# A graph attention network on one core: transposes of the normalised rows moved from TensorE to the DMA crossbar, with a new order of the softmax and GpSimd steps

## What is computed

```python
h = relu(layernorm0(x))                       # no scale, no shift
for l in range(3):
    si = h @ attn_w[l, :256];  sj = h @ attn_w[l, 256:]
    scores = leaky(si[:, :, None] + sj[:, None, :] + attn_b[l])     # slope 0.2
    attn = softmax(where(mask, scores, -inf))                       # mask = adj + identity > 0
    h1 = layernorm(h + attn @ h, g1[l], beta1[l])
    ff = gelu(h1 @ W1[l] + b1[l]) @ W2[l] + b2[l]                   # 256 -> 1024 -> 256
    h = layernorm(h1 + ff, g2[l], beta2[l])
out = x + h
```

## Time and profile before

| what | value |
|---|---|
| median of three runs | 2402.7 us |
| profiled execution, its own time | 2401.22 us |
| span of its trace | 2399.4 us |
| TensorE busy | 97% of the span |
| ScalarE / VectorE / GpSimd busy | 79% / 78% / 71% |
| mean granted TensorE clock | 0.995 of full speed |
| slots | 96, of about 24 us each |

### The profile page before, as it was taken

One profiled execution on the slowest core, in us unless ns is written; L12 is line 12 of the kernel. 1 busy time (PEld: TensorE's weight loads), 2 busy tenths in 40 slices (PEclk: granted clock), 3 DMA queues, 4 the chain that ended last, 5 costly groups with the idle time before them and its releaser, 6 DMA issues.

```text
span 2399.4 us, 47629 instructions
## 1 busy us (share of the span) xinstructions
PE 2333.0 (97%) x16608; PEld 1649.3 (69%) x16608; DVE 1869.7 (78%) x5974; ACT 1892.0 (79%) x3498; POOL 1698.2 (71%) x1543
## 2 busy tenths in 40 slices
PE   3999999999999999999999999999999999999997
PEld 2667777776666777777666777777766677777775
DVE  6887777777888777777888787878788877787874
ACT  4878787878888878787888877778788887878783
POOL 3567676768887666667887767676878776767686
PEclk9999999999999999999999999999999999999998
DMA  5200000001211000001121000000121100000012
GB/s 162 87 28 27 1 1 2 1 19 41 93 62 36 1 1 1 1 1 36 54 78 60 23 2 1 1 1 2 53 67 63 41 2 1 1 1 1 19 42 65
DMA packets 77421, 70.83 MB, mean 30 GB/s; under 512 B 7040, under 2 KB 75648, under 8 KB 77184
## 3 DMA queue, kind: packets, MB, share of 16 engines
q1 hardware_dynamic: 77184, 67.79, 9.1%
HBM read 51.01 MB, written 16.78 MB: 28 GB/s over the span
## 4 chain that ended last, share of the span: by engine, by line
PE 66%; POOL 16%; DVE 11%; ACT 3%; issue 2%; POOLq 0%; DVEq 0%
PE p_pair L380 29%; PE p_hid L366 28%; PE p_pair L422 4%; PE p_pair L432 2%; POOL rstd L786 2%; DVE dots L613 2%; DVE g_lo L572 2%; POOL w_f L835 2%; POOL h_res L798 2%; POOL h_res L800 2%; POOL norm L812 2%; DVE res L675 2%; POOL w_f L828 2%; POOL X_lo L804 2%; POOL w_f L826 2%
## 5 line engine op out<-in xcount | busy, mean ns | idle before, releaser
L380 PE MATMUL p_pair<-w_hi,g_hi 128*128 128x256 f16 x3072 | 837.6, 273 | 0.0
L380 PE MATMUL p_pair<-w_lo,g_hi 128*128 128x256 f16 x3072 | 837.6, 273 | 0.0
L380 PE MATMUL p_pair<-w_hi,g_lo 128*128 128x256 f16 x3072 | 837.5, 273 | 0.0
L572 DVE TENSOR_TENSOR g_lo<-p_hid,g_hi 128x512 f16<-128x512 f32 x768 | 528.6, 688 | 396.2 <-ACT g_hi L483 389.7
L478 ACT ACTIVATE p_hid<-p_hid,b_eff 128x512 f32<-128x512 f32 x768 | 504.5, 657 | 316.9 <-PE p_hid L366 315.7
L798 POOL TENSOR_TENSOR h_res<-norm,g_rows 128x1024 f32<-128x1024 f32 x96 | 227.7, 2372 | 384.0 <-DVE res L675 377.3
L483 ACT ACTIVATE g_hi<-p_hid 128x512 f16<-128x512 f32 x768 | 458.6, 597 | 24.4
L366 PE MATMUL p_hid<-hT_hi,w_hi 128*128 128x512 f16 x1536 | 458.2, 380 | 1.5 <-DVE g_lo L572 1.4
L366 PE MATMUL p_hid<-hT_hi,w_lo 128*128 128x512 f16 x1536 | 458.3, 380 | 0.0
L366 PE MATMUL p_hid<-hT_lo,w_hi 128*128 128x512 f16 x1536 | 457.9, 380 | 0.0
L786 POOL TENSOR_TENSOR rstd<-var_eps,minus_half 128x4 f32<-128x4 f32 x224 | 242.2, 1081 | 259.0 <-DVE minus_mean L587 253.7
(11 more groups left out here) (68 smaller groups left out, 3658.5 us busy)
## 6 DMA issues: line engine op xcount, KB each, us to landing
x_in<-in_x SPq DMA_DIRECT2D x32, 512.0 KB, 4.1
w_f<-in_x SPq DMA_DIRECT2D x32, 512.0 KB, 5.8
out<-w_f SPq DMA_DIRECT2D x32, 512.0 KB, 4.2
adj_in<-in_adj SPq DMA_DIRECT2D x32, 256.0 KB, 4.5
w_f<-in_L_gnn_W SPq DMA_DIRECT2D x6, 1024.0 KB, 6.1
attn_rows<-in_L_gnn_attn_w SPq DMA_DIRECT2D x1, 768.0 KB, 5.9
g_rows<-in_L_gnn_g SPq DMA_DIRECT2D x2, 384.0 KB, 7.5
b_rows<-in_L_gnn_b SPq DMA_DIRECT2D x1, 384.0 KB, 6.7
```

Of the source, the lines that this page charges most:

```text
L380: mm = pe.matmul(ff_banks(s)[:, t, :], g[i][:, nodes], w[l][:, c, :], start=(c == 0 and t % 2 == 0 and n == 0), stop=(c == C - 1 and n == ...
L572: dve.tensor_tensor(g_lo[i][:], p_hid[k][:], g_hi[i][:], ALU.subtract).then_inc(g_lo_ready, 1)
```

## The change

The rows `norm1` are no longer transposed by TensorE. ScalarE copies them to fp16 `h_hi` (`high_h`, after step 3), GpSimd subtracts to get `h_lo` (`low_h`), and SyncE issues one transposing DMA of 256 KB for each (`turn_h`), from SBUF to SBUF, into `hT_hi` and `hT_lo`. `transpose_norm1`, `high_hT` and `split_hT` are gone. The score rows and the transposed probabilities lie in the two banks of the pair that the aggregate of the same item will use; `p_att` is gone, and its bank holds `p_rows`, a PSUM copy of the two attention vectors of the layer, which `dot_products` reads; it is refilled once in eight items. In the order of the work: `spread_sj`, `add_scores` and `row_maxima` go from step 4 to step 3, `exponentials` from step 5 to step 4, `high_X` from step 3 to step 1, `norm_input` is for item s+4; on VectorE `feed_statistics` goes from step 3 to 4 and the `aggregates` behind it from step 4 to 5, `dot_products` to step 4 and item s+3, `input_statistics` to step 1 and item s+5 with its `aggregates` at step 2; GpSimd's slot has a new order. The first slot is -5 instead of -4.

```diff
-FIRST_SLOT = -4
+FIRST_SLOT = -5
...
+            def turn_h(r, s):
+                i = s % 2
+                if later(r, s, 2):
+                    sp.wait_ge(hid_psum, total(r, s - 2, C, C))
+                for h, hT, made, turned in ((h_hi, hT_hi, h_hi_ready, hT_hi_ready), (h_lo, hT_lo, h_lo_ready, hT_lo_ready)):
+                    sp.wait_ge(made, total(r, s, 1, 1))
+                    sp.dma_start_transpose(hT[i][:].rearrange("p t k n -> p (t k) n"),
+                                           h[:].rearrange("p t d -> p (t d)")).then_inc(turned, 16)
...
-                if is_item(r, s + 2) and layer_of(s + 2) == 0 and group_of(r, s + 2) + 2 < G:
-                    sp.wait_ge(x0_ready, group_total(r, s + 2, 4, 4))
-                    load_x(group_of(r, s + 2) + 2)
+                if is_item(r, s + 3) and layer_of(s + 3) == 0 and group_of(r, s + 3) + 2 < G:
+                    sp.wait_ge(x0_ready, group_total(r, s + 3, 4, 4))
+                    load_x(group_of(r, s + 3) + 2)
...
+                if is_item(r, s + 1):
+                    turn_h(r, s + 1)
...
-                    if c == 4 and is_item(r, s + 1):
-                        transpose_norm1(r, s + 1)
-                    if c == 4 and is_item(r, s + 2) and not first:
+                    if c == 3 and is_item(r, s + 2):
                         spread_sj(r, s + 2)
...
+            def high_h(r, s):
+                act.wait_ge(norm1_ready, total(r, s, 4, 4))
+                if later(r, s):
+                    act.wait_ge(hT_hi_ready, total(r, s - 1, 16, 16))
+                act.activation(h_hi[:], norm1[:], ACT.Copy).then_inc(h_hi_ready, 1)
...
-                    if c == 3 and is_item(r, s + 2):
+                    if c == 3 and is_item(r, s + 1):
+                        high_h(r, s + 1)
+                    if c == 1 and is_item(r, s + 2):
                         high_X(r, s + 2)
-                    if c == 4 and is_item(r, s + 1):
-                        high_hT(r, s + 1)
-                    if c == 5 and is_item(r, s + 2):
+                    if c == 4 and is_item(r, s + 2):
                         exponentials(r, s + 2)
...
+                if q == 0 and pair == 0:
+                    dve.tensor_copy(p_rows[:], attn_rows[:, l]).then_inc(rows_ready, 1)
...
+                    if c == 1 and starts and not late:
+                        input_statistics(r, s + 5)
+                    if c == 2 and starts and not late:
+                        aggregates(0, group_total(r, s + 5, 10, 8))
...
                     if c == 4 and is_item(r, s - 1):
+                        feed_statistics(r, s - 1)
+                    if c == 5 and is_item(r, s - 1):
                         aggregates(2, total(r, s - 1, 10, 8))
-                    if c == 5 and is_item(r, s + 1):
-                        split_hT(r, s + 1)
...
+                    if c == 4 and is_item(r, s + 3):
+                        dot_products(r, s + 3, 0)
+                        dot_products(r, s + 3, 1)
```

More of the change, by code:

```diff
@@ L192, in gnn_kernel @@
         h_res = [sb(f"h_res{i}", [P, T, D]) for i in range(2)]
-        hT_hi = [sb(f"hT_hi{i}", [P, KD, TN], F16) for i in range(2)]
-        hT_lo = [sb(f"hT_lo{i}", [P, KD, TN], F16) for i in range(2)]
+        h_hi, h_lo = sb("h_hi", [P, T, D], F16), sb("h_lo", [P, T, D], F16)
+        hT_hi = [sb(f"hT_hi{i}", [P, T, KD, N], F16) for i in range(2)]
+        hT_lo = [sb(f"hT_lo{i}", [P, T, KD, N], F16) for i in range(2)]
         g_hi = [sb(f"g_hi{i}", [P, TN], F16) for i in range(GS_RING)]
@@ L238, in gnn_kernel @@
         x0_ready = sem("x0_ready")
+        rows_ready = sem("rows_ready")
         dots_ready = sem("dots_ready")
@@ L409, in transpose_probs @@
                 for t in range(T):
-                    mm = pe.transpose(p_att[:, t, :], probs[:, t, :], ident[:])
+                    mm = pe.transpose(pT_bank(s)[:, t, :], probs[:, t, :], ident[:])
                 mm.then_inc(pT_psum, 1)
@@ L424, in aggregate @@
                 mm.then_inc(agg_ready, 1)
[L426 to L434, removed]
             def slot(r, s):
@@ L553, in slot @@
                         copy_probs(r, s + 2)
-                    if c == 7 and is_item(r, s + 3) and layer_of(s + 3) == 0:
-                        norm_input(r, s + 3)
+                    if c == 7 and is_item(r, s + 4) and layer_of(s + 4) == 0:
+                        norm_input(r, s + 4)
             slots(act, slot)
@@ L630, in add_scores @@
                 for t in range(T):
-                    dve.scalar_tensor_tensor(out=scores[:, t, :], in0=p_att[:, t, :], scalar=s_i[q][:, t:t + 1],
+                    dve.scalar_tensor_tensor(out=scores[:, t, :], in0=sj_bank(s)[:, t, :], scalar=s_i[q][:, t:t + 1],
                                              in1=mask[q][:, t, :], op0=ALU.add, op1=ALU.add).then_inc(score_steps, 1)
@@ L700, in slot @@
             def slot(r, s):
-                starts = is_item(r, s + 4) and layer_of(s + 4) == 0
-                late = isinstance(r, int) and (r, s) == (0, -3)
-                if isinstance(r, int) and (r, s) == (0, -2):
+                starts = is_item(r, s + 5) and layer_of(s + 5) == 0
+                late = isinstance(r, int) and (r, s) == (0, -4)
+                if isinstance(r, int) and (r, s) == (0, -3):
                     dve.wait_ge(attn_dma, 2 * 16)
@@ L711, in slot @@
                         dve.wait_ge(stat_steps[1], total(r, s + 1, 10, 4))
-                    if c == 4 and is_item(r, s - 1):
+                    if c == 5 and is_item(r, s - 1):
                         dve.wait_ge(stat_steps[2], total(r, s - 1, 10, 4))
-                    if c == 6 and starts and not late:
-                        dve.wait_ge(stat_steps[0], group_total(r, s + 4, 10, 4))
-                    if isinstance(r, int) and (r, s, c) == (0, -2, 3):
+                    if c == 2 and starts and not late:
+                        dve.wait_ge(stat_steps[0], group_total(r, s + 5, 10, 4))
+                    if isinstance(r, int) and (r, s, c) == (0, -3, 1):
                         dve.wait_ge(stat_steps[0], group_total(0, 1, 10, 4))
@@ L800, in h_residual, with low_h @@
                 pool.tensor_tensor(h_res[i][:], h_res[i][:], rows(res_rows, l, T), ALU.add).then_inc(h_res_steps, 1)
+            def low_h(r, s):
+                pool.wait_ge(h_hi_ready, total(r, s, 1, 1))
+                if later(r, s):
+                    pool.wait_ge(hT_lo_ready, total(r, s - 1, 16, 16))
+                pool.tensor_tensor(h_lo[:], norm1[:], h_hi[:], ALU.subtract).then_inc(h_lo_ready, 1)
             def low_X(r, s):
@@ L848, in slot @@
                     norm_feed(r, s - 1)
-                if is_item(r, s - 2) and layer_of(s - 2) == L - 1:
-                    skip_connection(r, s - 2)
-                if is_item(r, s + 4) and layer_of(s + 4) == 0:
-                    inverse_deviation(s + 4, 0, group_total(r, s + 4, 10, 10), group_total(r, s + 4, 2, 1))
-                if is_item(r, s - 1) and not (isinstance(r, int) and PER * r + s == ITEMS):
-                    layer_output(r, s - 1)
             slots(pool, slot)
```

99 lines of the change are left out of this document (44 added, 55 removed).

## The result

The changed kernel takes **2632.5 us** (median of 4 runs, 2632.05 to 2633.59) against 2402.7 us before (4 runs, 2402.35 to 2403.58): ratio 1.0958, 95% interval 1.0944 to 1.0972. The profiled execution took 2632.3 us, its span is 2630.5 us. The forecast was 2612 us, and slower.

What follows compares the result with a forecast made beforehand. TensorE (97% busy) was taken to bound short slots, GpSimd and VectorE long ones. New rings: 66 x 25.47 + 24 x 28.65 = 2368.6 against 2166.3, +202; start and end +8; 2401.2 + 210 = 2611, said 2612, range 2555 to 2740.

Steps and rivals of the forecast that it cites:

- TensorE's work: TensorE per slot: without the eight transposes (0.87 us per item), 23.9 us falls to 23.0 us.
- The ring of the quiet slots: ScalarE, VectorE, GpSimd: exponentials delay g_lo and second aggregates at step 5; no slot shorter than 25.5 us where it closes.
- N: Start of norm_attention in slot s, taken as time zero for the walk through the new order.
- The ring of the long slots: Eight slots of 24, item s+5 of layer 0: GpSimd's input deviation waits for VectorE's step 2 aggregates; 28.65 us.
- The sum: 90 h_res intervals, items 5 to 95: 66 x 25.47 + 24 x 28.65 = 2368.6 us, +202.
- 15 us of possible gain: Long slots before the change: seven in each of three periods, 0.7 us each, if nothing but TensorE bound.
- Start and end: Five slots before item 5, where weights are prepared, and the end: +8 us, between 0 and 25.
- The edits costed at nothing: spread_sj and probabilities in pair banks, PSUM dot products, high_X at step 1, SyncE loads: zero cost, waits cover them.
- low bound: Transposing DMAs land like a plain 256 KB load, 4.5 us; even one after the other, no cost.
- their rival: Transposing DMAs land late, TensorE waits at the first hidden matmul: 2690 if two us late, high bound 3000; chance 0.20.
- The one in which only TensorE's ring holds: GpSimd's tail is shorter; ring P, X_hi, low_X, deviation, N: 23.8 us in 66 intervals, about 2500 us; chance 0.06.
- The faster one: Exponentials at step 4 hide, TensorE sets 23.0 us everywhere: 2304 us; chance 0.09.

Runs made afterwards that it cites:

- D: Changed kernel with VectorE's second-normalisation aggregates ahead of g_lo of step 5, and GpSimd's low_X behind the first deviation, input deviation behind h_residual: 2327.5 us.
- A: Changed kernel with VectorE's aggregates of the second normalisation moved ahead of its g_lo of step 5: 2527.6 us.
- B: Changed kernel with GpSimd's deviation of the first normalisation (item s+1) moved ahead of the input's: 2565.3 us.
- J: D with the five broadcast row loads one slot earlier on SyncE and item 0's dot products moved forward: 2326.4 us.
- I: D with both dot products reading the attention rows from SBUF and the copy into PSUM removed: 2491.7 us.
- H: Changed kernel with the transpose of h_lo issued twice in a row, first into a spare tile, TensorE waiting for both: 2632.3 us.
- F: D with ScalarE's exponentials put back from step 4 to step 5: 2365.2 us.

## Why the prediction was right, and where it was off

**TensorE's work.** 23.9 - 0.87 = 23.0 us per slot: D shows 23.02 once nothing else binds.

**The ring of the quiet slots.** From N = 410.00 the links came at: gelu of step 3 +1.99 (forecast 1.98), h_hi done +4.19 (4.2), scores' maxima done +5.73 (5.76), gelu of step 5 +10.75 (10.74), its g_lo +12.15 (12.07), GpSimd's power +13.46 (13.39) after a wait of 2.32 (2.3). Slot 25.56 (25.47). Nothing in it is an average: each term was a row of the same operations in the old order, and so they added up. A removed the link, and this ring no longer set the slot.

**The ring of the long slots.** 28.49 (28.65); B opened it and the quiet slots did not move. The wait for the input's statistics, on which the walk rests, is there: 0.94 us ahead of the input's power.

**The sum.** 90 intervals: 2374.4 (2368.6). The 60 quiet slots are 0.1 us longer than I had them, the 24 long ones 0.15 shorter, and six slots that I counted as quiet take 26.27 us, two in each period (1462.99 to 1489.26). In reading the trace of before I said that seven slots of 24 are longer; they are eight, six of 24.67 us and two of 24.54, and only in the six has GpSimd both the skip connection and the input's deviation. The sum did not use this count, but the 15 us of possible gain there are 18. In the six slots of 26.27 us VectorE makes a mask and nothing is done for an input. GpSimd, then VectorE, of the changed kernel in such a slot:

```profile
1471.20 0.74 POOL L789 TENSOR_TENSOR shift<-minus_mean,rstd 128x4 f32<-128x4 f32 x1
1472.04 2.33 POOL L817 TENSOR_SCALAR norm<-res,rstd,shift 128x256 f32<-128x256 f32 x4
```

```profile
1471.21 0.66 DVE L605 CUSTOM_DVE_ANT_0 adj_in<-eye_i,adj_in 128x1024 uint16<-128x1024 uint16 x1
```

The shift takes 0.74 us instead of 0.20 and ends just behind the mask's operation, the norm 2.33 instead of 2.16: 0.71 us, which is the excess of these slots over 25.57. Six times that are 4 us on the ring.

**Start and end**, the term that was mis-sized: +8 (0 to 25), measured 31.4 - 8.4 = +23.0. I had counted only the five slots with weights. Those gave 14.5 (from item 0's h_res to item 5's: 149.5 against 135.0), but item 0's own h_res came 16.9 later, 62.33 against 45.43: TensorE's first work is at 28.5 instead of 19.0, and the first slot is one earlier (-5). That the added lead-in slot is the cause is argued, not shown: J brought TensorE's first work back to 18.4 and item 0's h_res by only 2.1 us. The 15 us by which this term was too small are the greater part of 2632 - 2612.

**The edits costed at nothing.** The dot products from PSUM took 474 and 417 ns on average (482 and 423 from SBUF before, where they stood elsewhere), X_hi was ready 1.5 us ahead of low_X (1.7 said), and TensorE was idle ahead of spread_sj for 19.8 us in all. What I did not see is what they were for: read from SBUF at their new place, the dot products cost 164 us in D's order (I).

**The transposes.** They landed after 3.1 us, below my low bound of 4.5, and their rival falls (H). 256 KB in 3.1 us are 85 GB/s, from issue to landing. The Trainium skill, Advanced Engine Details and Errata, section X-Bar Transpose (TRN2), has transposing DMAs as fast as copies; the trace does not speak against that, since the plain 256 KB loads from HBM landed after 4.4 us. Its 350 to 400 GB/s, by which the prediction made it under 1 us, are not reached at this size. The Trainium skill, VectorE: DVE Perf Modes, section The three transpose paths, gives 1309 ns for a 128x128 block; the eight of one DMA took 3.1 us together, so they do not follow each other at that price, and the 10.5 us that the prediction weighed do not arise.

**The rivals.** The one in which only TensorE's ring holds was put at 2500 and given 0.06; A has such slots (24.05 against 23.8, long ones 28.5). The faster one, at 2304 with the aggregates named as the link most likely to be loose, is what D comes to at 2327. Of the 23 us between the two, 18 are the 24 long slots, which take 23.78 us and not 23.0, and 3 are the start and end. Loosening that one link (A) was not enough for it; GpSimd's order had to change too. Both rivals name real rings, but neither was the time of the changed kernel, because the link they needed loose was there.

## What to carry to other kernels

When an order written out by hand changes, walk it: take one event as zero and follow each engine's next instruction through the slot until it comes round; the sum of a closed ring is the least length of a slot, whatever the shares say. A slow engine order is cheap to mend once the ring is known: moving a few small operations on two engines (the aggregates ahead of the hidden work; the two deviations to either side of the long subtractions) was worth 305 us here, some three times the 99 us that TensorE's saving could bring. And judge a part of a change inside the whole: the exponentials' new place cost 123 us before the orders were mended and was worth 38 us after.

## What the runs showed of the hardware

**VectorE and GpSimd hold each other up** where VectorE reads two operands from SBUF. In I a dot product waited out a whole GpSimd instruction (2.57 us instead of 0.42); with one operand in PSUM the dot products of D ran beside the same instructions and none took more than 0.48 us. GpSimd, which had begun first, lost little (its addition into h_res took 2411 ns on average in I, 2367 in D). In the changed kernel's mask slots (the rows in the section above) VectorE loses nothing: its mask, again two operands from SBUF, and GpSimd's small shift start within 0.01 us of each other, the mask takes its 0.66 us, and the shift is stretched from 0.20 to 0.74. In F both lose: the mask takes 1.82 us instead of 0.66, the operation behind it, which has one SBUF operand only, 1.38 instead of 0.43, and GpSimd's w_f addition 1.60 instead of 1.27. The Trainium skill, SBUF — State Buffer, section SBUF: two separate sides, calls this an exclusive lock that is held for the whole instruction, with the later one fully blocked; the trace agrees for I, where the blocked operation ends 0.3 us after GpSimd's. In F the mask, begun together with a GpSimd operation of 1.27 us, ended 0.54 us after it.

**Transposing DMAs** of 128 x 1024 fp16 within SBUF take 1.23 us of SyncE's queue each and land after 3.1 us with two per slot, 3.1 to 3.2 with three. They raise the packets from 77421 to 280170, of which 209792 are under 512 bytes, and queue q1's share of the DMA engines' time from 9.1% to 19.3%. The masks' 256 KB loads land as before (4.4 us, 4.5 in the earlier trace rows); the stores of 512 KB take 5.0 us instead of 4.2, and the trace puts no wait down to them.
